# Two graph layers with an expert choice: turns of the identity in TensorE's waits, and the last graph's route, fetches and banks put in another place

## The reference

```python
# layer 0: attention of 16 heads of 32 channels, adjacency as the bias
a = einsum('bhnd,bhmd->bhnm', q, k) * scale + (adj + adj)[:, None]
p = softmax(where(any(a != 0, -1), a, -inf));  p = where(isnan(p), 0, p)
x = layernorm(x + (p @ v) @ Wo.T)
# layer 1: one expert of four for each graph, batch norm over all graphs of an expert
scores = x.mean(axis=1) @ router_w + router_b;  top1 = argmax(scores)
out = adj @ (x @ expert_w[top1])
y = (out - mean[top1]) * rsqrt(var[top1] + eps) * gamma[top1] + beta[top1]
x = layernorm(x + relu(y))
```

## Time and profile before

| what | us |
|---|---|
| median of 3 runs | 2387.81 (2387.78 to 2389.49) |
| the profiled execution | 2387.94 |
| its span in the profile | 2386.2 |
| TensorE busy | 2190.9 (92%) |
| VectorE / ScalarE / GpSimd busy | 1663.0 / 1642.9 / 1747.5 |
| share of TensorE in the chain of waits that ended last | 77% |

### The profile page before, as it was taken

One profiled execution on the slowest core, in us unless ns is written; L12 is line 12 of the kernel. 1 busy time (PEld: TensorE's weight loads), 2 busy tenths in 40 slices (PEclk: granted clock), 3 DMA queues, 4 the chain that ended last, 5 costly groups with the idle time before them and its releaser, 6 DMA issues.

```text
span 2386.2 us, 48550 instructions
## 1 busy us (share of the span) xinstructions
PE 2190.9 (92%) x14496; PEld 1695.1 (71%) x14496; DVE 1663.0 (70%) x4296; ACT 1642.9 (69%) x3876; POOL 1747.5 (73%) x3196
## 2 busy tenths in 40 slices
PE   5789999999999999999999999999999999998864
PEld 3557777777767677777777777776767777776654
DVE  4576867677676767767686766767676776767468
ACT  3576767677676767667676767767776766767357
POOL 3678778777777878777787877777787877778224
PEclk8889999999999999999999999999999999999986
DMA  5887484756657475665657475665748566564877
GB/s 178 263 286 207 139 252 137 222 165 196 194 154 225 140 249 143 184 201 169 199 146 253 134 229 160 194 195 155 222 141 255 140 184 191 176 203 142 317 278 287
DMA packets 212900, 471.60 MB, mean 198 GB/s; under 512 B 40800, under 2 KB 48992, under 8 KB 205856
## 3 DMA queue, kind: packets, MB, share of 16 engines
q1 hardware_dynamic: 211872, 467.45, 63.3%
q10 hardware_dynamic: 768, 1.05, 0.2%
HBM read 269.11 MB, written 65.01 MB: 140 GB/s over the span
## 4 chain that ended last, share of the span: by engine, by line
PE 77%; DVE 9%; SPq 4%; issue 3%; ACT 3%; POOL 2%; DMA 1%; ACTq 0%; DVEq 0%; POOLq 0%
PE t_bank L392 16%; PE p_bank L292 13%; PE p_bank L293 13%; PE p_bank L294 13%; PE o_bank L411 10%; PE s_bank L370 8%; SPq L816 3%; DVE att L591 1%; PE p_bank L336 1%; DVE xt L645 1%; PE o_bank L402 1%; POOL fold L785 1%; DVE x L645 1%; ACT pt L551 1%; POOL fold L787 1%
## 5 line engine op out<-in xcount | busy, mean ns | idle before, releaser
L785 POOL TENSOR_TENSOR fold<-att 128x256 f32<-128x256 f32 x1024 | 771.0, 753 | 360.0 <-DVE nmax L591 261.3
L591 DVE CUSTOM_DVE_ANT_0 att<-s_bank,adj_t 128x512 f32<-128x512 f32 x1024 | 694.2, 682 | 389.9 <-PE s_bank L370 389.3
L485 ACT ACTIVATE att<-att,nmax 128x512 f32<-128x512 f32 x1024 | 738.0, 721 | 154.6 <-POOL fold L785 146.0
L551 ACT ACTIVATE pt<-t_bank 128x512 f32<-128x512 f32 x832 | 490.1, 595 | 375.7 <-PE o_bank L411 249.5
L392 PE MATMUL t_bank<-ident,att 128*128 128x128 f32 x4096 | 627.6, 276 | 21.0 <-ACT pt L551 16.2
L392 PEld LDWEIGHTS t_bank<-ident,att 128*128 128x128 f32 x4096 | 500.3, 141 | 201.0 <-issue 66.3
L787 POOL TENSOR_TENSOR fold<-fold 128x128 f32<-128x128 f32 x1024 | 497.1, 485 | 80.3
L370 PE MATMUL s_bank<-k_stack,q_stack 128*128 128x512 f32 x1024 | 497.2, 486 | 61.0 <-DVE nmax L591 46.9
L792 POOL TENSOR_TENSOR fold<-fold 128x64 f32<-128x64 f32 x1024 | 356.0, 348 | 80.2
L370 PEld LDWEIGHTS s_bank<-k_stack,q_stack 128*128 128x128 f32 x1024 | 197.2, 193 | 79.3 <-DVE nmax L591 62.9
L411 PE MATMUL o_bank<-pt,v 128*32 128x256 f32 x4096 | 248.4, 383 | 3.5 <-issue 2.7
(11 more groups left out here) (371 smaller groups left out, 3681.9 us busy)
## 6 DMA issues: line engine op xcount, KB each, us to landing
q_stack<-qk_t SPq DMA_DIRECT2D x1024, 64.0 KB, 3.6
k_stack<-qk_t SPq DMA_DIRECT2D x1008, 64.0 KB, 2.0
qk_w<-qk_split SPq DMA_DIRECT2D x121, 512.0 KB, 5.4
slot_a<-expert_split SPq DMA_DIRECT2D x16, 2048.0 KB, 8.0
slot_b<-vo_split SPq DMA_DIRECT2D x15, 2048.0 KB, 8.8
slot_a<-vo_split SPq DMA_DIRECT2D x15, 2048.0 KB, 9.7
stage<-in_xT SPq DMA_DIRECT2D x16, 1024.0 KB, 5.6
adj_t<-in_adj SPq DMA_DIRECT2D x64, 256.0 KB, 8.2
```

Of the source, the lines that this page charges most:

```text
L485: eng.activation(att[:, u % 4, j, :], att[:, u % 4, j, :], ACT.Exp, bias=nmax[:, u % 4, j:j + 1], scale=-1.0, accum_out=rsum[:, u % 4, j:j ...
L551: eng.activation(pt[:, j, :, (u % 2) * P:(u % 2 + 1) * P], t_bank[r % 2][:, :].rearrange("p (m n) -> p m n", m=NT), ACT.Copy).then_inc(act ...
L591: eng.tensor_tensor_reduce(out=att[:, u % 4, j, :], in0=s_bank[r % 2][:, :], in1=adj_t[:, t, :], scale=-2.0, scalar=3.0e38, op0=ALU.add, o ...
L785: eng.tensor_tensor(fold1[:, :], a[:, 0:256], a[:, 256:512], ALU.add).then_inc(pool_fold1, 1)
```

## The change

`pe_idle_turns` is new: it issues transposes of the 128 x 128 identity by itself, 128 x 128 f32 each, into a quarter of `o_bank[1]` that nobody reads. There are 20 of them before the first product of the program (behind the two waits for constants), 40 before `sum-` of the last graph, behind a wait for the low halves of `ot` (`dve_ot`), and 12 before its `M-` 0, ahead of the wait for the expert's weights. `plan` takes the last graph's `route-` out of its place behind `S-` 0 and puts it right behind the last chunk of `sum-`; since every engine takes its tasks from `plan`, DVE's work for the route moves with it. SP's wait for `O-` and fetches 6 and 7 move from slot 5 to slot 11, behind the expert's load of slot 10. `M-` 2 and 3 of the last graph go to `o_bank` 0 and 1 and wait for `dve_ot` in place of the bank's last reader.

```diff
+IDLE_TURNS = {("sum-", 0): 40, ("M-", 0): 12}
...
             if b < 0 and task in AHEAD[2:EARLY]:
                 return o_bank[AHEAD.index(task) - 2]
+            if b == B and task[0] == "M-" and task[1] >= 2:
+                return o_bank[task[1] - 2]
...
-            return [[c for c in step_chunks[HG * u + j] if present(c[0][0], *kind)] for j in range(HG)]
+            work = [[c for c in step_chunks[HG * u + j] if present(c[0][0], *kind)] for j in range(HG)]
+            if kind == TAIL:
+                work = [[c for c in step if c[0] != ("route-", 0)] for step in work]
+                for step in work:
+                    if (("sum-", 0), 3) in step:
+                        at = step.index((("sum-", 0), 3)) + 1
+                        step[at:at] = [(("route-", 0), c) for c in range(4)]
+            return work
...
+            elif c == 0 and b == B and name == "M-" and i >= 2:
+                wait(eng, dve_ot, b, PAIRS, 0)
...
+        def pe_idle_turns(eng, count):
+
+            for _ in range(count):
+                eng.transpose(o_bank[1][:, 2 * P:3 * P], ident[:, :], ident[:, :])
...
                 for task, c in work[j]:
+                    if b == B and c == 0 and task in IDLE_TURNS:
+                        if task[0] == "sum-":
+                            wait(eng, dve_ot, b, PAIRS, 0)
+                        pe_idle_turns(eng, IDLE_TURNS[task])
                     pe_chunk(eng, b, task, c, kind, kind_before)
...
-            if u == 5:
+            if u == 11:
                 wait(eng, pe["O"], b, NT, 0)
                 fetch(eng, 6)
                 fetch(eng, 7)
-            if u == 11:
                 wait(eng, dve_mean, b, 1, 0)
                 fetch_x1(eng, 12)
...
             eng.wait_ge(ld_const, 16)
+            pe_idle_turns(eng, 20)
             for task in AHEAD[:EARLY]:
                 pe_ahead(eng, task)
```

## The result

| | runs | median us | range us |
|---|---|---|---|
| before | 19 | 2387.27 | 2384.51 to 2389.87 |
| changed | 19 | 2382.61 | 2381.44 to 2387.49 |

The ratio is 0.9981, with a 95% interval of 0.9974 to 0.9988: 4.7 us faster by the medians and 4.5 by the means, clear of noise. Forecast were 2385.8 us and a range of 2383.2 to 2389.0, so the forecast was wrong: right in sign, too small, and the range ended 0.6 us above the time.

What follows compares the result with a forecast made beforehand. TensorE, busy 1929.62 of 2000 us mid-program, was left untouched; only the start and the last graph's serial products could change. From 2387.9 us, -3.6 at the last graph and +1.5 at the start gave 2385.8 us, range 2383.2 to 2389.0.

Steps and rivals of the forecast that it cites:

- 2.35 is nearer to the second, so I take a fall: Last graph, behind the 40 turns: 2.35 us of pause left, so the clock falls for 3.4 us, 2258.1 to 2261.5.
- The forecast for this part, -3.6 us: Last graph: last matmul of `M-` at 2284.7 against 2288.28 before, 3.6 us won; chance 0.48 for the whole forecast.
- rival 1: Clock stays up through the last graph's sums, -4.3 us, and the start's delay is absorbed: 2383.6 us; chance 0.17.
- the bracket: Two pauses in the earlier trace: after 1.95 us before `O-` the clock stayed up, after 2.55 us before `M-` it fell.
- The start: Program start: 20 turns put the first product 3.1 us later, a risen clock gives back 1.66 us: +1.5 us.
- The base: Starting point of the sum: the profiled execution's 2387.94 us, 0.1 over the median of 2387.81.
- The route and the load: Last graph: moved route has the expert's load issued at 2263.8, landing 7.74 us later at 2271.5.
- The 12 turns ahead of `M-`: Last graph: weights land 0.9 us before `S-` starts its last matmul, so these turns cost 1.3 us.
- the banks worth nothing: Last graph: two new banks for `M-` win nothing, since no pause of TensorE stood inside `M-` before.
- the fetches harmless: Fetches behind the load: fetch 6 in by 2280, first used at 2324.14; nothing lost or won but an empty queue.
- the final pass unmoved: Final pass: VectorE busy 19.72 of 20 us; keeps its length and moves as a whole with the end of `M-`.
- rival 2: All turns: turns of the identity don't hold or raise the clock, so slower, +1.1 us, 2389.0 us; chance 0.15.

Runs made afterwards that it cites:

- the pair of versions on one chip: Changed kernel without start and `M-` turns, 76 turns behind `M-`: with 60 sum turns, median 2380.78 us; with 40 sum turns and 20 start turns, 2381.40 us.
- 80 early: Changed kernel with 80 turns ahead of the wait for `router_b`'s load in place of the 20 behind it: 2382.35 us, ratio 0.9981 to before.
- best: Changed kernel without turns at the start and ahead of `M-`, with 76 turns between `M-` and the final pass: 2379.78 us, ratio 0.9972 to before.

## Why the prediction was wrong

**The clock behind 40 turns.** The step that failed: "2.35 is nearer to the second, so I take a fall". The pause is 2.25 us and the clock stayed up, in every profiled execution with 40 turns. The forecast for this part, -3.6 us, was mis-sized by it; D shrank by 4.4, which is rival 1's -4.3. The ends of the bracket are right (after 1.95 us up, after 2.55 down), but between ends 0.6 us apart the nearer one says little, and the part with the fall should have stood as an even chance. Worse, the bracket takes the length of the pause as all that counts. The trace of before speaks against that: in its long pause the clock fell after 2.2 us, inside the wait, while the fall at `M-` came only when the pause of 2.55 us was over (clock in the column before the last two):

```profile
2250.40:2252.60 2.20, 0.17 (x1) 0.00 (x0) 1.57 (x3) 0.21 (x1) 0.00 (x0) 1.00 1.05 387
2252.60:2257.20 4.60, 0.01 (x1) 0.04 (x1) 3.25 (x9) 2.48 (x6) 0.00 (x0) 0.50 1.05 387
2273.40:2276.40 3.00, 0.49 (x2) 0.48 (x3) 0.69 (x1) 0.59 (x1) 0.00 (x0) 1.00 0.92 364
```

And in the middle of the program the same pause of 1.84 us has a fall behind it in some graphs and none in others (last section). What else decides is open. That 2.25 us were harmless here is shown for this place, by thirteen executions, and is no threshold. Two slips in the prediction moved little: a fall "some 0.9 us after the restart as at `M-`" is 0.5 by the rows it names, and the range starts at 2383.2, though the middle of rival 1 is 2383.6 by its own sum.

**The start.** The mechanism was right: turns from 12.21, first product at 16.30, the clock up behind them, and a delay that is carried when it is large (40 and 60 turns). The size, +1.5, held at the first scores: 1.4 us by the means of eight and six executions. The totals show less: 0.6 us by the pair of versions on one chip. If one takes D's change from each total's distance to its before, by means, four kernels with 20 turns (the changed one and those without sum turns, without `M-` turns, with the old route) keep -0.1, +0.6, +0.6 and 0.0 us, five without (no start turns, 40 turns alone, 80 early, no turns, best) -0.4, -0.1, -0.3, -0.2 and -0.4, the final pass taken off for the best: a difference of 0.5 us, with a standard error of about 0.3. Whether a part of the 1.4 us is absorbed, or the spread hides it, is open: the two numbers are a good two standard errors apart. When `O-` begins, the same eight executions are 0.9 us behind the same six, with a standard error of 0.7.

**The base.** The sum was made on one execution of 2387.94 us. The median of 19 runs is 2387.27, so 0.7 us of the miss is the starting point. Together: 0.8 for the clock, 0.9 for what the totals don't show of the start, 0.7 for the base are 2.4 of the 3.2 us between 2385.8 and 2382.6. The second of these and the rest are within the spread of the totals; the first is shown by the traces.

**What held.** The route and the load: forecast issue 13.4 us and landing 21.1 us behind the end of `O-`, measured 12.6 and 20.5. The 12 turns ahead of `M-` as a cost of 1.3 us (1.31 by experiment), the banks worth nothing, the fetches harmless, the final pass unmoved. The fetch order was costed at nothing and is worth 0.3. That turns don't count for the clock is rival 2. For it the prediction cites the Trainium skill, "TensorE: Matmul & The Clock Gate", Part 4: PE-mode transpose, by which the full clock does not engage for transposes. The traces do not agree, and they decide: behind 20 turns the first products cost 0.23 each, and with 40 turns the clock is 1.00 through a wait in which it fell without them.

**Where the 4.4 us come from.** Turns alone take D from 48.87 to 46.67; route, fetches and banks alone to 46.53; both without the turns ahead of `M-` to 43.16, where the parts would give 44.33. They help one another: the turns bring `S-` forward and so open the wait for the weights, in which the clock falls; the moved load closes that wait; and without turns sums and `S-` are slow for so long that the weights are there before `M-` needs them.

## What to carry to other kernels

An engine whose clock follows its work should be given idle work only inside a wait, and so much of it that the rest of the wait is short; 20 turns in a 6.8 us wait were worth nothing, 40 were worth 3.3 us. Turns in front of work that is ready cost their length, 1.3 us for the 12 ahead of `M-`, less what a risen clock gives back: at the start 20 turns put the first product 2.8 us later and the first scores 1.4. Sum such edits over the whole serial stretch, since each one moves where the next wait falls. And where totals spread by more than the effect, a distance inside the trace between two fixed instructions can tell it from one execution, if kernels that share the stretch have been seen to repeat it, as D does within 0.06 us; the start to the first scores doesn't.

## What was not expected of the hardware

In the middle of the program, where the clock is 1.00 on average, single stretches of 3.4 us at the lower level come in different graphs from execution to execution. Their place in the work on a graph is the same. Once in each graph TensorE waits 1.84 us for `nmax`, which VectorE writes; 14 of these waits lie between 250 and 2160 us. The eighteen profiled executions have two to five low stretches there, 58 in all, and each begins between 0.1 us before and 2.1 us after the end of such a wait, 49 of them within 0.4 us of it. Behind the other waits of the same length the clock stayed up. The wait that ends at 664.79 in the changed kernel has a fall:

```profile
664.79 0.79 PE L382 MATMUL s_bank<-k_stack,q_stack 128*128 128x512 f32 x1 [1.84 <-DVE nmax L612]
665.64 0.77 PE L302 MATMUL p_bank<-xt,qk_w 128*128 128x512 f32 x1
666.20 0.63 PE L303 MATMUL p_bank<-xt,qk_w 128*128 128x512 f32 x1
```
```profile
664.00:668.00 4.00, 3.15 (x7) 2.21 (x8) 3.86 (x13) 3.15 (x8) 3.40 (x7) 0.60 0.42 101
```

The same wait of the same graph in the kernel before has none:

```profile
665.73 0.50 PE L370 MATMUL s_bank<-k_stack,q_stack 128*128 128x512 f32 x1 [1.84 <-DVE nmax L591]
666.58 0.47 PE L292 MATMUL p_bank<-xt,qk_w 128*128 128x512 f32 x1 [0.35 <-DVE xt L645]
```
```profile
664.00:668.00 4.00, 1.92 (x7) 1.38 (x8) 3.86 (x12) 3.68 (x10) 3.46 (x6) 1.00 0.44 106
```

So the length of a pause alone doesn't tell whether the clock falls. What does is not shown.

The changed kernel is 0.94 us ahead of the kernel before at this wait, and 0.12 us behind it at the same wait one graph later: the stretch costs it 1.1 us. The kernel before loses in the same way behind 255.8 us: the changed one reaches that graph's wait 0.65 us later (255.89 against 255.24) and the next one 0.88 us earlier (392.19 against 393.07). Two to five such stretches, at about 1.1 us each, are a good part of the 1.4 us spread of the totals. No turns were tried in these waits.
